# Attention scores: the second rope product on 64 rows, two query tiles in the two halves of the array

## What is computed

```python
# B, S, D = 4, 512, 512; H, NOPE, ROPE, VD, LORA = 16, 128, 64, 128, 128
q = (x @ wq).reshape(b, s, H, NOPE + ROPE)
q_nope, q_pe = (q[..., :NOPE], q[..., NOPE:])
c, k_pe = (ckv[..., :LORA], ckv[..., LORA:])
q_pe = _apply_rope(q_pe, cos, sin); k_pe = _apply_rope(k_pe, cos, sin)
k = jnp.concatenate([k_nope, jnp.broadcast_to(k_pe[:, :, None, :], (b, s, H, ROPE))], axis=-1)
qf = jnp.concatenate([q_nope, q_pe], axis=-1)
scores = jnp.einsum('bqhd,bkhd->bhqk', qf, k) * scale
scores = jnp.where(causal[None, None], scores, jnp.float32(-1e+30))
attn = jax.nn.softmax(scores, axis=-1)
o = jnp.einsum('bhqk,bkhd->bqhd', attn, v).reshape(b, s, H * VD)
```

## Time and profile before

| what | value |
|---|---|
| median of 3 runs | 1423.64 us (1423.6 to 1424.46) |
| the profiled execution | 1421.54 us, its span 1419.7 us |
| granted clock of TensorE, mean | 0.985 |
| TensorE busy | 1357.7 us, 96% |
| VectorE, ScalarE, GpSimd busy | 60%, 47%, 27% |
| matmuls | 7092 |

### The profile page before, as it was taken

One profiled execution on the slowest core, in us unless ns is written; L12 is line 12 of the kernel. 1 busy time (PEld: TensorE's weight loads), 2 busy tenths in 40 slices (PEclk: granted clock), 3 DMA queues, 4 the chain that ended last, 5 costly groups with the idle time before them and its releaser, 6 DMA issues. The chain is left out here.

```text
span 1419.7 us, 23230 instructions
## 1 busy us (share of the span) xinstructions
PE 1357.7 (96%) x7092; PEld 1140.3 (80%) x7092; DVE 858.7 (60%) x1761; ACT 670.4 (47%) x1551; POOL 381.8 (27%) x339
## 2 busy tenths in 40 slices
PE   6899998999999999999999999998998999989997
PEld 3666777888888888888888888886776888868885
DVE  5786754655666666666776566665574434434568
ACT  3333326666666666666666666662312223222232
POOL 0334453000003091030640123700042233322262
PEclk9999999999999999999999999998998999999998
DMA  9999877966677669685799766874635789887374
GB/s 294 374 388 339 299 282 270 361 202 228 200 269 266 224 226 321 207 318 196 269 365 368 244 225 196 295 292 174 248 127 200 280 304 331 304 329 258 128 241 136
DMA packets 160042, 375.59 MB, mean 265 GB/s; under 512 B 23144, under 2 KB 80556, under 8 KB 147680
## 3 DMA queue, kind: packets, MB, share of 16 engines
q1 hardware_dynamic: 144432, 314.34, 63.1%
q0 software_dynamic: 15536, 60.30, 11.9%
HBM read 245.84 MB, written 128.22 MB: 263 GB/s over the span
## 5 line engine op out<-in xcount | busy, mean ns | idle before, releaser
L1155 ACT ACTIVATE a_pr<-a_pr,a_stat 128x128 f32<-128x128 f32 (+3 forms) x256 | 142.0, 556 | 113.8 <-DVE a_stat L1226 113.5
L1326 PEld LDWEIGHTS a_psY<-a_pT,a_cv 128*128 128x128 f32 x768 | 124.9, 190 | 15.9 <-issue 2.1
L1226 DVE CUSTOM_DVE_ANT_0 a_pr<-a_psS,f_mask 128x128 f32<-128x128 f32 (+3 forms) x256 | 114.6, 487 | 31.4 <-PE a_psS L1314 31.0
L1326 PE MATMUL a_psY<-a_pT,a_cv 128*128 128x512 f32 (+3 forms) x768 | 131.2, 320 | 1.9 <-DVE a_pT L1245 1.9
L1161 ACT ACTIVATE a_pr<-a_pr,a_stat 128x128 f32<-128x128 f32 (+3 forms) x256 | 122.2, 548 | 0.0
L1171 ACT ACTIVATE a_oT<-a_psY 128x512 fp32r<-128x512 f32 x64 | 38.2, 598 | 151.0 <-PE a_psY L1326 151.0
L1256 DVE TENSOR_TENSOR n_acc<-a_psZ,n_acc 128x512 f32<-128x512 f32 x125 | 86.4, 691 | 35.2 <-PE a_psZ L104 33.0
L1240 DVE TENSOR_TENSOR a_oT<-a_psY,a_oT 128x512 fp32r<-128x512 f32 x64 | 44.2, 691 | 103.7 <-ACT a_oT L1171 103.7
L102 PE MATMUL a_psX<-a_hT,a_wqk 128*128 128x512 f32 (+1 forms) x256 | 100.3, 392 | 0.6 <-DVEq L1216 0.6
L103 PE MATMUL a_psX<-a_hT,a_wqk 128*128 128x512 f32 (+1 forms) x256 | 100.4, 392 | 0.0
L104 PE MATMUL a_psX<-a_hT,a_wqk 128*128 128x512 f32 (+1 forms) x256 | 100.1, 391 | 0.0
(11 more groups left out here) (354 smaller groups left out, 3469.6 us busy)
## 6 DMA issues: line engine op xcount, KB each, us to landing
w1s_d<-a_ws SPq DMA_DIRECT2D x72, 512.0 KB, 3.5
a_wqk<-wqk_d SPq DMA_DIRECT2D x64, 512.0 KB, 4.6
a_mh<-mhl_d SPq DMA_DIRECT2D x32, 1024.0 KB, 6.2
s_ring<-w1s_d SPq DMA_DIRECT2D x16, 2048.0 KB, 9.4
w2s_d<-a_ws SPq DMA_DIRECT2D x72, 256.0 KB, 4.0
qpe_d<-p_qs SPq DMA_DIRECT2D x16, 1024.0 KB, 5.1
a_rw<-in_L_ffn_rw SPq DMA_DIRECT2D x128, 128.0 KB, 3.5
a_qpe<-qpe_d SPq DMA_DIRECT2D x64, 256.0 KB, 2.7
```

The costliest lines, as they stand in the source:

```text
L1155: nc.scalar.activation(pr[i], pr[i], ACT.Exp, bias=nmax[:, i:i + 1], scale=-1.0, accum_out=rsum[:, i:i + 1]).then_inc(ex, 1)
L1226: nc.vector.tensor_tensor_reduce(out=pr[i], in0=score[i][:, 0:w], in1=mask[:, S - w:S], scale=-1.0, scalar=3e38, op0=ALU.add, op1=ALU.min, ...
L1326: m = nc.tensor.matmul(psY[:, q0:S], cv[:, j, cs], pT[:, ps, o:o + w], start=n == 0, stop=n == 11)
```

## The change

The product of the rope queries with the key's low part (L1314) leaves out the query's low part, so that it needs 64 rows and not 128. The rows of `qpe` are sorted anew: in the first two query tiles (tokens 0 to 255) the high kinds stand in rows 0 to 63 and the low kinds in rows 64 to 127, in the other two tiles the other way round. So tiles 0 and 1 multiply in the lower half of the array's rows and tiles 2 and 3 in the upper half. The four products of a head stand in front of its full products, in the order 3, 0, 2, 1, and the three latent products and the rope product with slice 0 follow for each tile. In the bank that tiles 0 and 1 share only the first of the two products starts an accumulation.

To bring the rows there, `q_high` and `q_low` are written as two instructions each, one for each half of the tokens, and `place` sorts the key's rows (in `store_k` and in the copy for the first batch). `load_q` reads the kinds as the outer index. The batch has to be known where the program is written, so TensorE's loops are cut at the batches (`batches=True`).

```diff
@@ -170,8 +170,8 @@
                      self.K.wqk_d[bass.ds(g % H, 1)].rearrange("a p s c n -> p (a s c n)")).then_inc(self.w_in[u], 16)
 
     def load_q(self, sp, g, u):
-        sp.dma_start(self.qpe[:, u].bitcast(F32), self.K.qpe_d.rearrange("b g (h r) k n -> (b g h) (r k) n", r=HALF)[bass.ds(g, 1)]
-                     .rearrange("a p n -> p (a n)")).then_inc(self.q_in[u], 16)
+        src = self.K.qpe_d.rearrange("b g (h r) k n -> (b g h) k r n", r=HALF)[bass.ds(g, 1)]
+        sp.dma_start(self.qpe[:, u].bitcast(F32), src.rearrange("a k r n -> (a k) r n")).then_inc(self.q_in[u], 16)
 
     def raw(self, sp, b, e, q, shared):
         g_, w_, d_ = ("sg", "sw1", "sw2") if shared else ("rg", "rw1", "rw2")
@@ -277,6 +277,9 @@
         in_s, out_s = [K.sem("w_in0"), K.sem("w_in1")], A.out_s
         tr, ev, mm, s_hi, s_lo = K.sem("w_tr"), K.sem("w_ev"), K.sem("w_mm"), K.sem("w_hi"), K.sem("w_lo")
 
+        place = lambda k: slice((k % 2 * 2 + k // 2) * HALF, (k % 2 * 2 + k // 2 + 1) * HALF)
+        SIDES = [(0, slice(0, S // 2)), (1, slice(S // 2, S))]
+
         def store_q(sp, b, g):
             sp.wait_ge(q_lo, b * NG + g + 1)
             sp.dma_start(K.qpe_d[batch(b), g].rearrange("p k n -> p (k n)"),
@@ -319,7 +322,7 @@
                              ck_[:, 0].rearrange("p s n -> p (s n)").bitcast(F32)).then_inc(out_k, 16)
                 sp.wait_ge(k_lo, b + 1)
                 for k in range(GH):
-                    sp.dma_start(K.kpe_d[batch(b), k::GH].rearrange("p s n -> p (s n)"),
+                    sp.dma_start(K.kpe_d[batch(b), place(k)].rearrange("p s n -> p (s n)"),
                                  ck_[k * HALF:(k + 1) * HALF, 1].rearrange("p s n -> p (s n)").bitcast(F32)).then_inc(out_k, 16)
 
             def store_c(b):
@@ -381,7 +384,7 @@
                 A.raw(sp, i, 0, i, False)
             sp.wait_ge(k_lo, b + 1)
             for k in range(GH):
-                sp.dma_start(A.kpe[k::GH, 0].rearrange("p s n -> p (s n)").bitcast(F32),
+                sp.dma_start(A.kpe[place(k), 0].rearrange("p s n -> p (s n)").bitcast(F32),
                              ck_[k * HALF:(k + 1) * HALF, 1].rearrange("p s n -> p (s n)").bitcast(F32)).then_inc(k_in, 16)
             store_q(sp, b, 0)
             sp.wait_ge(out_q[0], 16 * (b * NG // 2 + 2))
@@ -402,8 +405,10 @@
 
             def q_low(b, g):
                 pool.wait_ge(q_hi, b * NG + g + 1)
-                nc.gpsimd.tensor_tensor(qs[:, g % 2, 1::2], qr[:, g % 2], qs[:, g % 2, 0::2].bitcast(F32),
-                                        ALU.subtract).then_inc(q_lo, 1)
+                for s, n in SIDES:
+                    m = nc.gpsimd.tensor_tensor(qs[:, g % 2, 2 - 2 * s:4 - 2 * s, n], qr[:, g % 2, :, n],
+                                                qs[:, g % 2, 2 * s:2 * s + 2, n].bitcast(F32), ALU.subtract)
+                m.then_inc(q_lo, 1)
 
             nc.gpsimd.memset(X.half[:, :], -0.5).then_inc(X.pch, 1)
             pool.wait_ge(X.pch, 1)
@@ -433,7 +438,9 @@
             def q_high(b, g):
                 act.wait_ge(rot, b * NG + g + 2)
                 act.wait_ge(out_q[g % 2], (b * 2 + g // 2) * 16 + 16)
-                nc.scalar.activation(qs[:, g % 2, 0::2], qr[:, g % 2], ACT.Copy).then_inc(q_hi, 1)
+                for s, n in SIDES:
+                    m = nc.scalar.activation(qs[:, g % 2, 2 * s:2 * s + 2, n], qr[:, g % 2, :, n], ACT.Copy)
+                m.then_inc(q_hi, 1)
 
             def take(h):
                 act.wait_ge(tr, h + 1)
@@ -515,7 +522,9 @@
         def last_query(act):
             act.wait_ge(rot, B * NG + 1)
             act.wait_ge(out_q[1], B * NG // 2 * 16)
-            nc.scalar.activation(qs[:, 1, 0::2], qr[:, 1], ACT.Copy).then_inc(q_hi, 1)
+            for s, n in SIDES:
+                m = nc.scalar.activation(qs[:, 1, 2 * s:2 * s + 2, n], qr[:, 1, :, n], ACT.Copy)
+            m.then_inc(q_hi, 1)
 
         def vector(dve):
             ch = Chain(dve, dch)
@@ -977,7 +986,7 @@
         DBL = (10, 12)
         EARLY = DBL[0] * 4
 
-        def run(eng, pair, norms=False):
+        def run(eng, pair, norms=False, batches=False):
 
 
             def two(m, phase, n=None):
@@ -987,7 +996,11 @@
             for i in range(4):
                 pair(i, i % 2, i, False, 0, None)
             QB = PAIRS // 2
-            if not norms:
+            if batches:
+                for b in range(B):
+                    with eng.Fori(max(b * QB, 2), min(b * QB + QB, B * QB - 1)) as m:
+                        two(m, b)
+            elif not norms:
                 with eng.Fori(2, DBL[0]) as m:
                     two(m, 0)
                 for m in range(*DBL):
@@ -1298,20 +1311,25 @@
                     split3(nc, psX[:, :], [(wqk[:, u, 0, c], wqk[:, u, 1, c], h_(c, 0), h_(c, 1))
                                            for c in range(DC)]).then_inc(qp, 1)
 
-                def scores(g, u):
+                def scores(g, u, b):
                     pe.wait_ge(landed, g // H + 1)
                     pe.wait_ge(q_lo, g + 1)
                     pe.wait_ge(q_in[u], (g // 2) * 16 + 16)
+                    for i in (3, 0, 2, 1):
+                        w = (i + 1) * P
+                        side = slice(i // 2 * ROPE, i // 2 * ROPE + ROPE)
+                        nc.tensor.matmul(score[i][:, 0:w], qpe[side, u, i * P:(i + 1) * P],
+                                         kpe[side, b % 2, 1, 0:w],
+                                         start=i != 1, stop=False)
                     for i in range(TB):
                         w = (i + 1) * P
                         q = slice(i * P, (i + 1) * P)
                         out = score[i][:, 0:w]
                         k_ = lambda src, s: src[:, bass.ds((g // H) % 2, 1), s, 0:w].rearrange("p a n -> p (a n)")
-                        nc.tensor.matmul(out, qT[:, 0, q], k_(cT, 0), start=True, stop=False)
+                        nc.tensor.matmul(out, qT[:, 0, q], k_(cT, 0), start=False, stop=False)
                         nc.tensor.matmul(out, qT[:, 0, q], k_(cT, 1), start=False, stop=False)
                         nc.tensor.matmul(out, qT[:, 1, q], k_(cT, 0), start=False, stop=False)
-                        nc.tensor.matmul(out, qpe[:, u, q], k_(kpe, 0), start=False, stop=False)
-                        nc.tensor.matmul(out, qpe[:, u, q], k_(kpe, 1), start=False, stop=True).then_inc(sc, 1)
+                        nc.tensor.matmul(out, qpe[:, u, q], k_(kpe, 0), start=False, stop=i > 0).then_inc(sc, 1)
 
                 def values(g):
                     pe.wait_ge(landed_c, g // H + 1)
@@ -1345,14 +1363,15 @@
                     split3(nc, dst, [(oT[:, v * 2 + u, 0, q], oT[:, v * 2 + u, 1, q], mh[:, v, u, 0], mh[:, v, u, 1])
                                            for u in range(2)]).then_inc(ot, 1)
 
-                def pair(n, v, early, last, *_):
+                def pair(n, v, early, last, phase, _):
+                    b = n // PAIRS if isinstance(n, int) else phase
                     for u in range(2):
                         g = n * 2 + u
                         if u:
                             out = (lambda t: output(n - 1, 1 - v, t)) if early else (lambda t: None)
                         else:
                             out = (lambda t: output(n - 2, v, 2 + t)) if early > 1 else (lambda t: None)
-                        scores(g, u)
+                        scores(g, u, b)
                         out(0)
                         if not (last and u):
                             qproj(g + 1, 1 - u, g)
@@ -1367,7 +1386,7 @@
                 pe.sem_inc(ot, 1)
                 qproj(0, 0, 0)
                 pe.wait_ge(*rotated)
-                run(pe, pair)
+                run(pe, pair, batches=True)
                 values(B * H - 1)
                 for i, (n, t) in enumerate(rest):
                     output(n, n % 2, t, ends[i % 2], 1 if i else 0)
```

## The result

The changed kernel takes **1441.76 us** (median of 4 runs, 1440.91 to 1444.59) beside 1423.62 of the kernel before on the same chip: a ratio of 1.0132, with a 95% interval of 1.0108 to 1.0155. Slower, as forecast, 18.1 us instead of 12.6, and inside the range. Two executions of all, one of e2 and one of the kernel before, took 3445 and 3742 us at full clock and are left out of every ratio; e2 has only that profile, of which the counts alone are used.

A forecast was written before the change was run, and what follows sets the result against it. TensorE was taken as the bound, busy 702.72 of 705 us mid-stretch. Profiled 1421.5 + 12.2 (64 heads) + 0.4 (front) = 1434.1, as median 1436; own range 1428 to 1441, full range 1409 to 1446.

The forecast's parts named there:

- Sign: Whole kernel: slower, chance 0.70, against 0.18 for faster and 0.12 for same.
- A change of shape: TensorE going between 128 and 64 rows: 0.09 emptying plus 0.11 exposed load, 0.20 us each, two a head.
- Rival (1): 64-row block on TensorE: no emptying at its ends, products overlap, -0.21 us a head, 1410.6 us; chance 0.17.
- rival (3): 64-row block on TensorE: 64 rows behave as 128, four products swapped for four, 1424 us; chance 0.10.
- The block, 0.44 us: Four 64-row products per head: halves overlap, loads 0.11 us apart, 0.44 us in all.
- A head: TensorE per attention head: 0.40 + 0.44 - 0.65 = +0.19 us, +12.2 us over 64 heads.
- the removed product: Second rope product (L1314) on TensorE: taking it out saves 0.65 us a head.
- Nothing waits for them unless they slow fourfold: Rope query DMAs: same pieces and bytes, asked for two heads ahead, landing in 2.7 us; cost nothing.
- The front, +0.4 us: Split high and low query instructions on ScalarE and GpSimd: two exposed groups at 0.18 us, +0.4 us.
- VectorE's softmax: VectorE in each head: last pass still released by the last product, so no loss.

The follow-up runs named there:

- e2: The changed kernel with rope queries sorted by kind in DRAM, four stores per group (one per kind) and one contiguous load per head; 1534.06 us, ratio 1.0782.
- g0: The changed kernel with a head's rope queries loaded by two DMAs of 64 rows, slowest index 32, rows in pairs; 1438.43 us, ratio 1.0108.
- g1: The kernel before with the new row order and two 64-row load DMAs, keeping the full 128-row second rope product; 1427.58 us, ratio 1.0029.
- g7: g0 with query tiles 2, 1, 0 in the lower row half and tile 3 alone in the upper; 1432.82 us, ratio 1.0076.
- f3: The changed kernel with queries stored by head and loaded contiguously, and all four 64-row products in the lower half; 1461.43 us, ratio 1.0250.
- g5: g0 with each tile's 64-row product in front of its own last full product, eight changes of shape a head; 1518.55 us, ratio 1.0670.
- e4: The changed kernel without the four 64-row products, high x low rope part left out; 1408.63 us, ratio 0.9905.
- e1: The changed kernel with the full 128-row second rope product back in place of the 64-row block; 1438.19 us, ratio 1.0105.
- e6: The kernel before with only `load_q` taken from the changed kernel; 1436.14 us, ratio 1.0105.

## Why the prediction was right, and where it was not

**Sign and time.** Slower was given 0.70. The forecast was 1436 with a range of its own from 1428 to 1441; 1441.76 lies just above that, and inside 1409 to 1446. Two mistakes hide in it, a small one in the block, in its favour, and a larger one in the DMAs. (A change of 0.15 to 0.24 us, from which that range was said to come, gives 1430 to 1441 by the prediction's own sum; its lower end was set 2 us too low.) The sign is not luck: the block alone, g0 over g1, costs 10.85 us, with the load on 4 engines in neither.

**A change of shape, 0.20 us each: right.** It was read off 32-row products in the router, and 64 rows behave alike. Going in, 0.203 us from the last transpose to the first 64-row product, in after, g0, g7 and f3 alike. For coming back the sum had 0.09 of emptying and 0.11 of load: in after, tile 2's 384 columns (0.16 us at 2.4 GHz) are through at 0.50, the first full product comes at 0.605, and the second 0.163 behind it instead of 0.11, so 0.16 in all. In g5 a pair of changes is 0.40 at 512 columns. Rival (1) needed a change below 0.10 and rival (3) none at all, and both fall by these rows.

**The block, 0.44 us: the overlap right, the way to it wrong.** I spaced the four by loads that follow each other at 0.11. The loads of the two halves run side by side (0.004 apart), so loads were no bound between halves. Inside a half the opposite showed. The second product of a half starts not when the columns of the first are through, but 0.11 to 0.12 later: tile 2 at 0.339 - 0.002 - 0.213 = 0.12, tile 1 at 0.169 - 0.005 - 0.053 = 0.11, tile 1 behind tile 2 in g7 at 0.279 - 0.160 = 0.12. Both errors together come out even: from the last transpose to the second full product it is 0.97 us, against 0.17 before, so +0.80 for the 0.84 of the sum.

**A head: +0.163 for +0.19**, 10.5 us in 64 heads for the 12.2. The medians say the same without the trace: g0 is 10.85 us above g1. The price of the removed product, 0.65 us, is 0.60 by e4.

**"Nothing waits for them unless they slow fourfold": the step that failed.** The DMAs were priced at nothing, with the argument that pieces and bytes are the same and the landing two heads ahead. Both are true, and neither is what the load costs. I had looked at the size of a piece and not at the order of the indices, by which the DMA is dealt out to engines, and I had looked only at who waits for this load, not at what else runs on the 4 engines that it now fills. The load itself lands 2.5 times later, at 6.7 us, short of the fourfold that the prediction allowed. The stores and loads beside it land a quarter to three quarters later. TensorE's longest wait in the attention is where the DMA engines are fullest (before shows a DMA share of 1.05 from 740 to 762 us), and a stretch of low clock follows it. Its size: after minus g0, 3.3 us, for the form of the load; g1 minus before, 4.0, for what of the layout remains with 16 engines. With the block, 10.85 + 3.3 + 4.0 = 18.1, the measured difference; it must be, as the three are steps of one chain of kernels.

That split is one order of subtraction. In the other, e1 over before is 15 to 17 us and after over e1 only 3.6. In a third, g7 less the block's pace (0.123 us in 64 heads) leaves only 1.5 us for the layout with 16 engines. The parts don't add, since a kernel whose heads are longer by 0.16 us meets the crowded places with more slack (after loses 0.5 us around head 5, where e1 loses 6.4), and since the stretches of low clock differ from kernel to kernel (none to 10.2 us around head 44) by no rule that these runs show. So the load's cost is shown in its sign (by e6, by e1 and by g1 against e1), and its size only to some microseconds.

**The front, +0.4 us: no harm.** GpSimd takes 2.54 us for two of 512, as said. ScalarE takes 1.15 for its two, not 1.09. The last projection's products and the first of the attention (L102) come at 212.52 instead of 212.30, +0.2. Some 1.3 us more are lost until head 2 and are not in the sum. The granted clock goes to 1.2 GHz at 228.6 us for 6.8 us instead of 3.4 (before, at 227.8), which alone is up to 1.7 us. It stayed down for 6.8 us in g0 and g7 too, and for 3.4 in g1. I tried nothing on what sets it.

**VectorE's softmax: right.** Its wait for the last product (L1239 <- L1332) is 27.3 us in all instead of the 31.0 of the earlier trace rows. TensorE's own waits between 250 and 740 us are 0.9 us in all, none of them for the softmax, so no pass was late for it.

## What to carry to other kernels

A product of half the rows in a stream of full ones pays 0.29 to 0.40 us here for the two changes of the array's shape, 0.40 being the time of nearly two full products of 512 columns. What has to win that back is the overlap of products that stand together, and here four of them (0.76 us with the changes) do not replace four full ones (0.60). When a DMA's rows are put in another order, look at the slowest index of both sides first: its count sets how many engines move it, and the fall from 16 to 4 shows in the count of 4-byte packets and in the landing times of the transfers beside it, before anything waits for the DMA itself. In a stage that runs at the bound of one engine, read pace (the difference of two kernels over 28 quiet heads) and jumps apart; the pace repeats within 0.02 us a head, the jumps don't. Take a jump apart too, into the wait and the time at the lower clock behind it: around head 44 the second was nearly all of the loss in the changed kernel and in g1.

## What the runs showed of the hardware that I had not expected

- Weight loads for the two row halves of the array start 4 ns apart, and products in them 3 ns apart; the loads of the full products of a head's scores start 0.11 us apart.
- A later product can start ahead of an earlier one of the other half: tile 1 at 0.169, tile 2 at 0.339, in all of 41 heads looked at.
- A second 64-row product in the same half starts 0.11 to 0.12 us after the first one's columns are through, where full products of 512 columns follow each other at 0.23 us, 0.02 more than their columns take. It is the second product alone: the third of a half in g7 started 0.01 behind, and in f3, with all four in one half, the gaps were 0.13, 0.01 and 0.07. What makes it is open.
- A DMA whose slowest index counts 4 comes with 4 packets of 4 bytes, by the counts, and one that counts 32 or 128 with 16. Its semaphore is raised 5 times, the first time at 1.0 us and long before the data. SyncE gives the reordered load out in 0.59 us instead of 0.33.
- The length of a pause of TensorE does not tell the low clock behind it. Around head 44 one pause of 2.9 us was followed by 10.2 us at 1.2 GHz (after) and one of 3.2 by 6.8 (g1), but two with 2.6 the longest by none (g7), and two of 0.8 and 1.5 us in the kernel before by none either.
